# Decoder layer on one core: self-attention scores as three products of rounded operands and rests, with two batches' rows kept in DRAM until the cross attention

## The reference

```python
x = layernorm(x + self_attention(x))        # 16 heads of 64, rotary q and k, causal
x = layernorm(x + cross_attention(ctx, x))  # 5 sampled places a head, 77 context rows
x = layernorm(x + ffn(x))                   # fake-quantised gate, up and down

scores = jnp.einsum('bhqd,bhkd->bhqk', q, k)           # q and k after the rotation
scores = jnp.where(causal[None, None], -jnp.inf, scores)
attn = jax.nn.softmax(scores / math.sqrt(64), axis=-1)
out = jnp.einsum('bhqk,bhkd->bhqd', attn, v)
```

## Time and profile before

| what | value |
|---|---|
| median of three runs | 2134.17 us |
| the profiled execution, its own time | 2131.5 us |
| its span | 2129.6 us, mean granted clock 0.939 |
| self-attention | start to about 1347 us |
| cross attention and feed forward | from about 1348 us to the end |
| PE busy over the span | 1856.8 us (87%) |
| DVE, POOL, ACT busy | 1527.3, 1502.5, 1318.1 us |

### The profile page before, as it was taken

How to read it: one execution, slowest core, us unless ns; L and a number is a source line. 1 busy time by engine, 2 the same in 40 slices (tenths; PEclk the granted TensorE clock), 3 DMA queues, 4 the chain that set the end, 5 groups by cost and what they waited for, 6 DMA issues and landing times. The chain is left out here.

```text
span 2129.6 us, 43322 instructions
## 1 busy us (share of the span) xinstructions
PE 1856.8 (87%) x17259; PEld 1128.9 (53%) x17259; DVE 1527.3 (72%) x2162; ACT 1318.1 (62%) x1802; POOL 1502.5 (71%) x1154
## 2 busy tenths in 40 slices
PE   6889999999999999999999997688898898883575
PEld 3445545555555555555555543666676676662332
DVE  6866867867878867878867853446677777678676
ACT  3556656666666666666666663177877868882466
POOL 0766867877867877867877866169597978646446
PEclk8999999999999999999999999789999999996885
DMA  7022223213222212223212110200000000100002
GB/s 228 23 50 70 61 50 70 52 39 70 53 58 71 51 40 70 53 58 71 53 39 70 40 37 26 67 2 8 3 8 2 3 3 13 35 2 1 3 1 79
DMA packets 57512, 92.40 MB, mean 43 GB/s; under 512 B 25312, under 2 KB 35552, under 8 KB 53344
## 3 DMA queue, kind: packets, MB, share of 16 engines
q1 hardware_dynamic: 48096, 89.36, 16.4%
q10 hardware_dynamic: 9216, 0.27, 0.2%
HBM read 51.33 MB, written 4.46 MB: 26 GB/s over the span
## 5 line engine op out<-in xcount | busy, mean ns | idle before, releaser
L947 POOL TENSOR_TENSOR acc<-acc,probs 128x1024 f32<-128x1024 f32 (+3 forms) x320 | 585.0, 1828 | 104.5 <-ACT probs L650 74.0
L650 ACT ACTIVATE probs<-psum 128x1024 f32<-128x1024 f32 (+3 forms) x384 | 290.6, 812 | 162.8 <-PE psum L501 160.7
L594 ACT ACTIVATE chunks<-psum 128x1024 bf16<-128x1024 f32 x288 | 282.0, 1026 | 123.5 <-PE psum L460 78.0
L1523 ACT ACTIVATE onehot<-psum 128x1024 bf16<-128x1024 f32 x320 | 324.4, 1045 | 0.0
L493 PE MATMUL psum<-operands 64*128 64x512 f32 (+3 forms) x1536 | 308.7, 513 | 17.4 <-ACT chunks L594 16.9
L801 DVE TENSOR_REDUCE lows<-chunks 128x2 f32<-128x1024 bf16 (+1 forms) x224 | 266.8, 1217 | 73.2 <-ACT chunks L594 63.3
L517 PE MATMUL psum<-probs,vals 128*64 128x512 f32 (+3 forms) x1536 | 295.4, 502 | 22.6 <-POOL probs L926 12.1
L1353 PE MATMUL psum<-pieces,onehot 128*128 128x64 bf16 x7680 | 281.0, 197 | 14.7 <-ACT vs L1530 13.3
L1353 PEld LDWEIGHTS psum<-pieces,onehot 128*128 128x128 bf16 x7680 | 262.1, 101 | 48.4 <-issue 24.3
L926 POOL TENSOR_SCALAR_AFFINE_SELECT probs<-probs 128x256 f32<-128x256 f32 x256 | 147.3, 592 | 127.7 <-ACT probs L650 127.7
L1994 POOL TENSOR_TENSOR vs<-vs,wgt 128x1280 f32<-128x1280 f32 x64 | 151.8, 2373 | 108.8 <-DVE wgt L1770 105.3
(11 more groups left out here) (241 smaller groups left out, 3424.3 us busy)
## 6 DMA issues: line engine op xcount, KB each, us to landing
operands<-turned SPq DMA_DIRECT2D x124, 256.0 KB, 5.1
rden<-inverse_rows SPq DMA_DIRECT2D x64, 256.0 KB, 3.9
raw<-in_wqk SPq DMA_DIRECT2D x30, 256.0 KB, 4.3
y<-in_x SPq DMA_DIRECT2D x1, 4096.0 KB, 17.9
wo<-in_wo SPq DMA_DIRECT2D x16, 256.0 KB, 2.6
out<-res SPq DMA_DIRECT2D x16, 256.0 KB, 2.1
raw<-in_wv SPq DMA_DIRECT2D x15, 256.0 KB, 4.4
raw<-in_xT SPq DMA_DIRECT2D x12, 256.0 KB, 4.0
```

The source lines that it names most:

```text
L594: nc.scalar.activation(chunks[k % MBUF][:, :, :], slot("max", n, c)[:, :, :], ACT.Copy, scale=-1.0)\
L650: nc.scalar.activation(probs[u % PBUF][:, :, 0:width], slot("s", n, u)[:, :, 0:width], ACT.Exp, scale=1.0 / D ** 0.5).then_inc(s_exp, 1)
L947: G.tensor_tensor(dst, dst, src, ALU.add).then_inc(s_acc, 1)
L1523: A.activation(onehot[:, n % 2, k, :], bc[m % 2], ACT.Relu).then_inc(s_oh, 1)
```

## The change

Two things, in one diff.

First, the scores. A pair's `operands` are rounded by ACT into new tiles `high` (two of them, 8 KB a partition each), in two halves by token (`high_operands`), and DVE subtracts the rounded tile from the operands, in place, so that `operands` then hold the rests (`low_operands`, also two halves). `scores` makes three F32R products per head, high by high, high by rest, rest by high, in place of one F32 product; `max_chunk` reads `high` in place of `operands`. Both new functions run for pair n + 1 in step 0 of pair n: on ACT after the exponentials and `copy_out` of that step and ahead of its weight splits and stagings, on DVE after the step's `rotate` and splits and ahead of the next step's maxima. For pair 0 they stand in the prologue.

Second, the rows. In place of `y` there is `ends`, two batches big (16 KB a partition), during the self-attention. Batches 0 and 1 are loaded at the start; once a batch's rows are normalised (in groups 7 and 11) SP stores them in DRAM (`kept`) and loads batch 2 or 3 in their place. The cross attention loads the two kept batches back into a new tile (`inner`) and takes the batches in the order 2, 0, 1, 3.

```diff
+ROWS_ORDER = [2, 0, 1, 3]
+KEPT = 2
+        high = [sb(f"operands_high{n}", [P, 2, S], F32R) for n in range(2)]
-            sp.dma_start(y[:, :, :], dram["x"].rearrange("b (t p) e -> p (b t) e", p=P)).then_inc(s_y, 16)
+            def load_rows(b):
+                sp.dma_start(batch_tiles(b, 0, TT), dram["x"][b].rearrange("(t p) e -> p t e", p=P)).then_inc(s_y, 16)
+
+            for b in range(2):
+                load_rows(b)
@@ the loop of SP over the groups, at its end
                 spread_inverses(n)
+                if i % NG == NG - 1 and 0 < i // NG <= KEPT:
+                    b = i // NG - 1
+                    sp.wait_ge(s_ax1, 2 * (b + 1))
+                    sp.dma_start(kept[b], batch_tiles(b, 0, TT)).then_inc(s_keep, 16)
+                    sp.wait_ge(s_keep, 16 * (b + 1))
+                    load_rows(b + KEPT)
@@ max_chunk
                 if n == 0 and c == 0:
-                    pe.wait_ge(s_top, 16 * STACK_DMAS)
+                    pe.wait_ge(s_ohi, 1)
                 if c == (2 if n == 0 else 0):
-                    pe.wait_ge(s_ops[p], 16 * STACK_DMAS * (n // OBUF + 1))
+                    pe.wait_ge(s_ohi, 2 * (n + 1))
@@ scores
+                if u == 0:
+                    pe.wait_ge(s_olo, 2 * (n + 1))
                 wait_slot(pe, "s", n, u)
                 dst = slot("s", n, u)
                 kt, hf, a, width = span(u)
-                for hh, rows in enumerate(HEADS):
-                    nc.tensor.matmul(dst[:, hh, 0:width], ops[n % OBUF][rows, 1, kt * P:(kt + 1) * P].bitcast(F32),
-                                     ops[n % OBUF][rows, 0, a:a + width].bitcast(F32), start=True, stop=False)
+                hi, lo = high[n % 2], ops[n % OBUF]
+                for term, (k, q) in enumerate(((hi, hi), (hi, lo), (lo, hi))):
+                    for hh, rows in enumerate(HEADS):
+                        nc.tensor.matmul(dst[:, hh, 0:width], k[rows, 1, kt * P:(kt + 1) * P], q[rows, 0, a:a + width],
+                                         start=term == 0, stop=False)
@@ ACT
+            def high_operands(n, half):
+
+                if n == 0 and half == 0:
+                    act.wait_ge(s_top, 16 * STACK_DMAS)
+                else:
+                    act.wait_ge(s_ops[n % OBUF], 16 * STACK_DMAS * (n // OBUF + 1))
+                if n >= 2:
+                    act.wait_ge(s_s, NU * (n - 1))
+                nc.scalar.activation(high[n % 2][:, :, HALVES[half]], ops[n % OBUF][:, :, HALVES[half]].bitcast(F32),
+                                     ACT.Copy).then_inc(s_ohi, 1)
                     if m == 0 and n:
                         copy_out(n - 1, 1)
+                    if m == 0 and n + 1 < PAIRS:
+                        for half in range(2):
+                            high_operands(n + 1, half)
@@ DVE
+            def low_operands(n, half):
+                x, hi = (t[:, :, HALVES[half]] for t in (ops[n % OBUF], high[n % 2]))
+                dve.wait_ge(s_ohi, 2 * n + half + 1)
+                V.tensor_tensor(x, x.bitcast(F32), hi.bitcast(F32), ALU.subtract).then_inc(s_olo, 1)
                             low_v(k)
+                    if m == 0 and n + 1 < PAIRS:
+                        for half in range(2):
+                            low_operands(n + 1, half)
@@ cross_attention
+            for n in range(KEPT):
+                sp.dma_start(y[1 + n], kept[n]).then_inc(s_back[n], 16)
                 if b == LATE:
                     pe.wait_ge(s_x1, 1)
+                elif b and i == 0:
+                    pe.wait_ge(s_back[b - 1], 16)
-            st.then(V.tensor_reduce(hidden.ytop[:, 0:1], y[:, 0:(XB - 1) * TT, :], AX.XY, ALU.max,
-                                    apply_absolute_value=True))
+            for b in range(XB - 1):
+                st.done(V.tensor_reduce(hidden.ytop[:, b:b + 1], y[b], AX.XY, ALU.max, apply_absolute_value=True))
```

More of the change, by code:

```diff
@@ L147, in splits_at, with attention @@
     return {0: pieces[:KT], 1: pieces[KT:2 * KT], LAST_CHUNKS: pieces[2 * KT:3 * KT], STEPS - 1: pieces[3 * KT:]}.get(m, [])
-def attention(nc, dram, y, psum):
+def attention(nc, dram, ends, psum, kept):
     ctx = ExitStack()
@@ L291, in wait_slot, with batch_tiles @@
                 pe.wait_ge(s_drow, n + 1)
+        def batch_tiles(b, first, last):
+            return ends[:, b % KEPT * TT + first:b % KEPT * TT + last, :]
         def span(u):
@@ L459, in max_chunk @@
                     for hh, rows in enumerate(HEADS):
-                        last = nc.tensor.matmul(dst[:, hh, col:col + width], ops[p][rows, 0, qt * P:(qt + 1) * P],
-                                                ops[p][rows, 1, hf * BANK:hf * BANK + width], start=True, stop=True)
+                        last = nc.tensor.matmul(dst[:, hh, col:col + width], high[n % 2][rows, 0, qt * P:(qt + 1) * P],
+                                                high[n % 2][rows, 1, hf * BANK:hf * BANK + width], start=True, stop=True)
                 last.then_inc(s_m, 1)
@@ L1364, in transpose_x1 @@
                 for t in range(2):
[L1365 removed]
+                    last = nc.tensor.transpose(dst[:, t, :], y[b][:, 2 * tp + t, kt * P:(kt + 1) * P], ident[:, :])
                 last.then_inc(s_x1T, 1)
@@ L2157, in token_tiles, with row_tiles, out_tiles @@
             return slice(first, first + 2)
+        def row_tiles(m):
+            t = token_tiles(m).start % TT
+            return slice(t, t + 2)
+        def out_tiles(m):
+            b, t = divmod(token_tiles(m).start, TT)
+            return slice(ROWS_ORDER[b] * TT + t, ROWS_ORDER[b] * TT + t + 2)
         @block.sync
@@ L2375, in statistics @@
                 dve.wait_ge(s_agg, m + 1)
-            st.then(V.tensor_reduce(hidden.ytop[:, 1:2], y[:, (B - 1) * TT:B * TT, :], AX.XY, ALU.max,
+            st.then(V.tensor_reduce(hidden.ytop[:, B - 1:B], y[B - 1], AX.XY, ALU.max,
                                     apply_absolute_value=True))
@@ L2463, in decoder @@
     with ExitStack() as ctx:
-        y = ctx.enter_context(nc.sbuf_tensor("y", [P, B * TT, E], F32))
+        ends = ctx.enter_context(nc.sbuf_tensor("outer_rows", [P, KEPT * TT, E], F32))
         psum = ctx.enter_context(nc.psum_tensor("psum", [P, 8, BANK], F32))
-        attention(nc, dram, y, psum)
+        kept = [nc.dram_tensor(f"kept_rows{n}", (P, TT, E), F32).ap() for n in range(KEPT)]
+        attention(nc, dram, ends, psum, kept)
+        inner = ctx.enter_context(nc.sbuf_tensor("inner_rows", [P, KEPT * TT, E], F32))
+        y = [ends[:, 0:TT, :], inner[:, 0:TT, :], inner[:, TT:, :], ends[:, TT:, :]]
         hidden = hidden_weights(nc, ctx)
-        cross_attention(nc, dram, y, psum, hidden)
+        cross_attention(nc, dram, y, psum, kept, hidden)
         feed_forward(nc, dram, out.rearrange("b (t p) e -> p (b t) e", p=P), y, psum, hidden)
```

39 lines of the change are left out of this document (23 added, 16 removed).

## The result

The changed kernel takes 2170.99 us (median of four runs, 2170.03 to 2174.94); the kernel before takes 2133.77 us (median of four). The ratio is 1.019 (95% interval 1.017 to 1.021): slower. The forecast was 2167 us. The profiled execution took 2170.95 us, its span is 2169.2 us.

A forecast was written before the change was run, and what follows sets the result against it. PE was taken to bound all pairs, with DVE and POOL right behind in even ones. 2131.5 + 23 (steady pairs) - 2 (pairs 30, 31) + 12 (start) = 2164.5 us profiled, 2167 as median; range 2147 to 2186.

The forecast's parts named there:

- The bound and the odd pairs: Self-attention: odd pairs bound by PE with 14 us of DVE to spare, each gaining 0.95 us.
- rival (3): Scores on PE: the two heads' F32R products don't run side by side, over 5 us a pair, beyond 2290; chance 0.03.
- the difference between a quarter and the fifth: Scores: three of four passes would save a quarter, rows say a fifth of widest tiles; the rest, one more weight load.
- The subtraction's price: DVE's two subtractions a pair: 1.8 us each, 3.6 us together, bounds 2.4 and 5.7, lengthened while POOL works.
- Even pairs: Subtractions ahead of the maxima delay the weighing and all behind it by 2.6 us a pair, bounds 1.0 and 4.0.
- the chain through POOL: Even pairs: DVE's `rotate`, POOL's `turn` and masks, PE's weighing, 0.2 us of slack; chunk copies' delay said to be less.
- Rival (4): Exclusive port costs DVE and POOL fully: subtractions near 2.5 us, even pairs +3.8, odd gain gone, 2196 us; chance 0.15.
- Pairs 0 and 1: Pair 0 +2.3 us from subtractions; pair 1's scores 12.5 us later behind ACT's wait for operands, 3.8 of it counted before.
- The start: Prologue, pair 0 and pair 1 together: +12 us, bounds 8 and 17.
- The rows: Storing and reloading batches through DRAM: taken as nothing, 0 to 3 us.
- The steady part: Pairs 2 to 29: 14 even ones at +2.6 and 14 odd ones at -0.95, together +23 us.

The follow-up runs named there:

- the products alone: Kernel before with three F32R products per score tile, second and third with zero weights, no rounding or subtracting: 2120.5 us, ratio 0.995.
- the run with the masks first: Changed kernel with POOL's `turn` moved behind the two masks of step 4 in even pairs: 2173.4 us, ratio 1.020 to the kernel before.

## Why the prediction was right

**The bound and the odd pairs.** The forecast took odd pairs as bound by PE with DVE to spare, and PE's gain as 0.95 us. Right in kind, measured 0.6 in a typical pair (39.9 to 39.3, in the products alone too) with PE busy 0.85 us less; on average over the fourteen 0.5, half of what the sum took. Where the difference between PE's 0.85 and the pair's 0.6 goes, I did not follow. A step of a 512 and a 384 wide tile took 1.60 us in the earlier trace rows; in after, at 435.99, it is 1.34 us (437.33 less 435.99), with 0.34 us for the first term of the wide tile, its weight load in it, and 0.23 or 0.24 for the others:

```profile
435.99 0.51 PE L515 MATMUL psum<-operands_high 64*128 64x512 f32 x2
436.33 0.40 PE L515 MATMUL psum<-operands,operands_high 64*128 64x512 f32 x2
436.57 0.40 PE L515 MATMUL psum<-operands_high,operands 64*128 64x512 f32 x2
436.80 0.34 PE L515 MATMUL psum<-operands_high 64*128 64x384 f32 x2
...
437.33 0.56 PE L523 MATMUL psum<-bias,first_rows 64*128 64x512 bf16 x4
```

The forecast's figures give 1.31 us for this step. The two heads run side by side; rival (3) is out (its own figures, by width over all twelve tiles, add up to under 5 us a pair, not over). The forecast lays the difference between a quarter and the fifth that its rows give to one more weight load; its 0.69 us held no weight load, so that does not follow.

**The subtraction's price.** Taken at 1.8 us, between 1.2 and 2.9; measured 1.79 on average over 64 of them:

```profile
L797 DVE TENSOR_TENSOR operands<-operands,operands_high x64: 1218/1422/2851, 51.1 to 1312.2; 128x1024 fp32r<-128x1024 f32 x64
```

The mean was right partly by luck, as the reason given with it was half wrong: I expected the long ones in the full even pairs. In pair 8 both take 1.4 us, in most odd pairs one takes 1.4 and the other 2.3, the same in each. What an instruction pays goes by its place in the pair's order, and so by which add of POOL it meets, more than by how busy the pair is.

**Even pairs.** +2.6 forecast, +2.8 measured on average; 2.0 in pairs 4, 8 and 16, which only rotate and kept a granted clock of 1.00, 3.4 to 3.9 in five others, all with the clock at 0.96 or 0.92. So at full clock the late DVE was worth less than forecast, and the clock, which the sum of the even pairs left out, made up for it. Weighing 35.6 us in, second rotation ended 32.5 us in (32 to 33.5 forecast). No subtraction, no loss: that step is shown. The step that failed is the sentence that the chunk copies "come to less than the chain through POOL": the run with the masks first shows a second chain that is as late, maxima, chunk buffer, ACT's copy, PSUM slot, scores. With it falls the reading that in the kernel before the weighing waits for the masks. It did not matter for the sum, because both were some 2 us late; it would have mattered to anyone who repaired the one I named. A second consequence that I missed: as even pairs were not held by PE's scores before, they gained next to nothing from the products (553.0 against 553.6 us), so that the change could win only in the odd ones, about 8 us.

**Rival (4)** said that the port costs both engines. POOL's busy time did grow, by 59 us over the same 1154 instructions, about 0.9 us for each subtraction. But the subtractions were not near 2.5 us, and the odd pairs kept their gain.

**Pairs 0 and 1.** The start came to 13.7 us where the terms gave 12.5 and the sum took 12, for partly wrong reasons. Pair 0 lost 5.3 us in place of 2.3: its two subtractions took 4.6 us, not 3.6, and none of it came back (the pair takes 35.4 us without them); its granted clock was 0.92, from 1.00, and PE was busy 2.3 us more than without them. In pair 1 the wait of ACT for the operands' DMA, 14.94 us, was found where it was forecast; the price was 4 us and 3 of clock in this execution, where the sum had 8.7, and moving it brought 2.0. The sum also had a slip: it put everything 5 us later at the landing, but took 3.8 off for the same delay at the end; with 3.8 in both it comes to 7.5.

**The rows** cost 0, as taken; the run with them alone shows it.

**What offsets what.** The steady part was 32 us in place of 23, and the 6 us that cross attention and feed forward were shorter in this execution stand against it. The hit is closer than the terms, and that is luck: a hit within 4 us, with the steady part 9 off.

**Open.** No kernel here takes the products' gain without the subtractions' loss: the best arrangements of the full change are 0.6% slower than the kernel before. The full split without the rows' part was not tried: SBUF has no room for `high` beside the full `y`. Nor was a fourth chunk buffer, for which there is no room either, and which would be the direct proof of the second chain. Nor were POOL's adds cut short in the kernel before, which would say how much of the 72 us the change has to do with. Which chain each pair other than the ones read here follows, I did not settle.

## What to carry to other kernels

Before work is put on an engine with spare time, ask what stands behind it in that engine's order: extra work ahead of the maxima cost its full time in even pairs, and still 1.2 us of 1.75 in odd pairs with 10 us to spare; behind the maxima it cost the even pair nothing, and the next pair 0.8 us. When a late engine feeds the bound one by two routes, taking one link away and finding no change is the test that shows the second; look for waits that end on buffers, not only for the last one in the chain. And two engines that block each other hide waits in busy time: the same instructions, 38.4 us of DVE in one kernel, were 29.7 us with the other engine's adds cut short.

## What the runs showed of the hardware

DVE and POOL pass a delay back and forth. Two DVE instructions moved across the border of a pair cost POOL 1.8 us, POOL's shifted add cost DVE's splitting 1.2 us, and eighteen us into the pair the next meeting cost a maximum of DVE 1.4 us. Delays of DVE in this kernel are therefore not additive: they can grow on the way to PE, or come back, as the rotation's 2.1 us did. The subtractions' durations are not spread, they come in steps (1.2, 1.4, 2.3, 2.8 us); I read each as one way to meet POOL. And a stretch of the same work took 39.7 or 42.6 us of PE's busy time by the granted clock (0.92 or 0.86) from one execution to another, 3 us in a single pair, which is as much as an experiment on that pair was looking for. The same holds for even pairs that wait more: PE was busy 22 us more over fourteen of them, for the same matmuls, where the granted clock lay under 1.00 in ten.
